# A four-layer graph network on one core: fourteen unread products per double step of the first layer

## The reference, cut to what matters

```python
h = jnp.maximum(_layernorm(x, axis=-1), 0.0)
# _L0_gnn_ref
msg = feat[src] * weight[:, None]
neigh_sum = jax.ops.segment_sum(msg, dst, num_segments=n)
deg = jax.ops.segment_sum(jnp.ones_like(weight), dst, num_segments=n)
h_neigh = neigh_sum / jnp.maximum(deg, 1.0)[:, None]
rst = feat @ W_self.T + b_self + (h_neigh @ W_neigh.T + b_neigh)
```

```python
d = jax.nn.gelu(layer_norm(x @ Wd1 + bd1, g1, b1), approximate=False)
d = jax.nn.gelu(layer_norm(d @ Wd2 + bd2, g2, b2), approximate=False)
```

## Time and profile before

| | us |
|---|---|
| median of 3 runs | 2665.58 |
| lowest and highest | 2657.37, 2678.04 |
| profiled execution, whole | 2675.34 |
| its span | 2673.3 |
| mean granted clock of TensorE in it | 0.738 |

### The profile page before, as it was taken

The page is one execution under the profiler, slowest core; times in us unless marked ns, Lnnn a source line. Parts: engine busy times, 40 slices in busy tenths (PEclk is TensorE's granted clock), DMA queues, the critical chain, the costliest instruction groups (busy, mean ns, idle before and its releaser), DMA issues.

```text
span 2673.3 us, 23453 instructions
## 1 busy us (share of the span) xinstructions
PE 1639.0 (61%) x7115; PEld 1239.3 (46%) x7115; DVE 1546.5 (58%) x2419; ACT 898.5 (34%) x1160; POOL 1327.1 (50%) x1404
## 2 busy tenths in 40 slices
PE   1456545545564365666567346878878634988892
PEld 1334334433453354544455234656656523767672
DVE  5445445544565376667677663555545834867783
ACT  1122122212221455555554312333333720433340
POOL 6545544554523545555555345554552034566653
PEclk7666666666665677777787767888988556989996
DMA  6112211211121344444444422323322621333332
GB/s 137 36 53 58 55 49 52 63 50 52 53 69 34 82 132 125 139 124 139 138 137 134 127 55 52 68 61 69 67 60 64 207 59 36 84 77 83 87 78 55
DMA packets 216506, 220.61 MB, mean 83 GB/s; under 512 B 107262, under 2 KB 170195, under 8 KB 216147
## 3 DMA queue, kind: packets, MB, share of 16 engines
q1 hardware_dynamic: 167635, 147.32, 18.6%
q0 software_dynamic: 45024, 58.36, 10.9%
q10 hardware_dynamic: 3744, 13.63, 1.3%
HBM read 117.72 MB, written 101.46 MB: 82 GB/s over the span
## 4 chain that ended last, share of the span: by engine, by line
PE 28%; issue 11%; DVE 11%; another core or an unknown queue 10%; ACT 7%; POOL 2%; DMA 1%; DVEq 0%; POOLq 0%; ACTq 0%; SPq 0%
PE psum L974 18%; POOL arena L655 2%; PE psum L999 2%; PE psum L1005 1%; DVE spare L1896 1%; DVE scan_ring L1896 1%; ACT arena L1204 1%; ACT arena L1231 1%; ACT arena L1283 1%; PE psum L1066 1%; DVE arena L1762 1%; PE psum L881 1%; PE psum L988 1%; ACT spare L1242 1%
## 5 line engine op out<-in xcount | busy, mean ns | idle before, releaser
L622 POOL DMA_INDIRECT gathered<-table,idx x1272 | 1210.1, 951 | 1084.0 <-issue 366.8
L1729 DVE COPY_PREDICATED spare<-spare,psum 64x512 f32<-64x512 uint8 x294 | 216.4, 736 | 282.6 <-ACT spare L1330 188.7
L974 PE MATMUL psum<-rounded 128*128 128x512 f32 x1144 | 299.6, 415 | 59.4 <-issue 38.1
L759 PE MATMUL psum<-ident,arena 128*128 128x128 f32 x416 | 109.7, 415 | 279.3 <-ACT arena L1121 265.5
L974 PEld LDWEIGHTS psum<-rounded 128*128 128x128 f32 x1144 | 225.5, 200 | 118.6 <-issue 53.1
L1567 DVE TENSOR_REDUCE rs<-arena 128x16 f32<-128x1024 f32 x52 | 63.3, 1217 | 341.3 <-ACT arena L1125 323.8
L759 PEld LDWEIGHTS psum<-ident,arena 128*128 128x128 f32 x416 | 70.8, 208 | 354.6 <-ACT arena L1121 284.1
L655 POOL DMA_INDIRECT arena<-scan,rowidx x100 | 103.3, 1033 | 213.3 <-DMA scan<-ea 111.8
L1125 ACT ACTIVATE arena<-psum 128x1024 f32<-128x1024 f32 x52 | 53.2, 1023 | 458.6 <-remote 350.3
L1330 ACT ACTIVATE spare<-psum 64x512 f32<-64x512 f32 x82 | 48.4, 590 | 397.5 <-remote 209.0
L1204 ACT ACTIVATE arena<-psum 128x512 f32<-128x512 f32 x156 | 82.0, 597 | 199.2 <-remote 160.8
(11 more groups left out here) (275 smaller groups left out, 3483.9 us busy)
## 6 DMA issues: line engine op xcount, KB each, us to landing
scan<-arena SPq DMA_DIRECT2D x52, 768.0 KB
scan<-ostage SPq DMA_DIRECT2D x130, 256.0 KB, 2.3
gathered<-table,idx POOLq DMA_INDIRECT x1272
d_mlp<-arena ACTq DMA_DIRECT2D x26, 512.0 KB
arena<-d_mlp SPq DMA_DIRECT2D x52, 256.0 KB
ea<-in_edge_attr SPq DMA_DIRECT2D x104, 128.0 KB
spare<-src_row SPq DMA_DIRECT2D x98, 128.0 KB
spare<-src_quarter SPq DMA_DIRECT2D x98, 96.0 KB
```

The lines of the kernel that those rows point to most:

```text
L622: pool.indirect_dma_start(out=out[:, j, hf, :], out_offset=None, in_=tab[layer], in_offset=bass.IndirectOffsetOnAxis(ap=idx[:, j, hf * NCH ...
L759: last = nc.tensor.transpose(P[:, 4, j::J], mlp[layer][:, k * CH + j * 128:k * CH + (j + 1) * 128], ident[:, :])
L974: last = nc.tensor.matmul(P[:, bank + t, :], parts[layer][n][:, b:b + 2, :].rearrange("p b d -> p (b d)"), tile(layer, m, u)[:, hf * CH:(h ...
L1729: picked = v.copy_predicated(rows[m % 2][halves[hf], :], quarter[m % 2][halves[hf], q - 1, :], P[halves[q % 2], bank + q // 2, :])
```

## The change

A helper is added to TensorE's program. One call of it issues n products of the identity with the identity, repeated to 256 columns, into columns 0 to 255 of a bank. Nothing reads them, and each bank is filled anew by the transposes that come next.

```diff
+            def keep_busy(n, bank):
+                for _ in range(n):
+                    nc.tensor.matmul(P[:, bank, 0:256], ident[:, :], ident[:, :].unsqueeze(1).to_broadcast([128, 2, 128]),
+                                     start=True, stop=True, skip_group_check=True)
...
             def l0_in(i, k):
+                pe.wait_ge(S("scanned", 1 - k), n_scanned(0, i + k))
+                if k == 0:
+                    keep_busy(2, 5)
                 pe.wait_ge(S("L0 msg made", k), past(i + 1))
-                pe.wait_ge(S("scanned", 1 - k), n_scanned(0, i + k))
                 for j in range(J):
...
                     pe.wait_ge(S("gelu made"), past(g))
+                keep_busy(4, 4)
                 pe.wait_ge(S("norms1 made"), i + 1)
                 norm_transpose(0, 0)
                 l0_in(i, 0)
...
                     norm_transpose(1, 0)
+                pe.wait_ge(S("evacuated", 1), n_evacuated(0, i))
+                keep_busy(6, 6)
                 l0_in(i, 1)
...
                 l0_hist(i)
+                keep_busy(2, 6)
                 l0_out(i, 0)
```

## The result

The kernel with the change takes 2758.22 us (median of 4 runs, 2751.41 to 2763.53) beside 2661.47 us for the kernel before on the same chip (4 runs): a ratio of 1.0352, interval 1.0317 to 1.0386. It is 97 us slower. The forecast was 2785, or 119 us slower.

The account below looks back on a forecast made before the run. A ring of waits bounds the first layer's loop, 29.3 us a double step. Six products on it cost 103 us, uncovered double steps 15: 118 us on the 2665.6 median gives 2784, said as 2785; range 2680 to 2930.

Parts of the forecast that it names:

- the first case: The forecast as described: the change slows the kernel to 2785 us, own range 2690 to 2810; chance 0.50.
- The ring: First layer's loop: gather batch, late TensorE semaphore, TensorE's start, message k = 1, next batch; 28.1 to 30.3 us.
- The price of one product: Each added 256-column product on TensorE: 0.94 us at the low clock, 0.5 us at the high one.
- Six products on the ring: Four into bank 4, two into bank 5, behind TensorE's start: 5.7 us, less 1.5 slack in 19 double steps; 103 us.
- what the clock gives back: An earlier clock rise could shorten the six products and two transpose blocks; lower bound 0.7 us a double step, not taken.
- A granted clock that is high right behind the start: Sign in the profile after, right behind TensorE's start, that the ring is not as described; 0.5 was expected there.
- The scan waits for the message transposes nearly always: Expected in the profile after: VectorE's scan waits for L767 23 times, some 90 us.
- Eight products at nothing: Six into bank 6, two behind the counts: hidden under gathers, costing nothing; double steps without a batch cost 15 us together.
- The double step: Expected in the profile after: one double step of the first layer's loop takes 33.5 to 35 us, against 29.
- Held earlier: Rival: late semaphores follow the amount of TensorE work, so the last gelu is held too; 138 us more, 2923; chance 0.25.
- The clock wins: Rival: products in idle time keep TensorE's clock at 1.00, saving 4.5 to 5 us a double step; about 2570; chance 0.15.
- Nothing moves: Rival: unseen slack in the ring, TensorE's start and batch shift against each other; 2665 to 2685 us; chance 0.10.

Follow-up runs that it names:

- the narrow products: The change plus the explicit wait, its fourteen products 16 columns wide instead of 256: 2705.04 us beside 2628.34 for the kernel before, ratio 1.0270.

## Why the prediction was right, point by point

The sign, the place and most of the size came out as the first case had it: 2758 us, inside its own range of 2690 to 2810, 27 us below the number.

**The ring.** Right for the change, where TensorE's semaphore is released 3.0 to 3.2 us behind the last gather in every double step; in the kernel before it came ahead of the batch's end in 3 of 22. The kernel before with an explicit wait for the batch's end takes the same time (1.0004), and the added time is GpSimd's wait for the message, 311.3 against 219.4 us, in the same 23 places.

**The price of one product.** Right at the low clock: 3.78 us for four in the timeline at 584.30, 0.94 each, as worked out from the halves of the earlier trace rows; 0.48 to 0.5 behind the rise (the last six, 2.85 us at 595.22 in the same double step).

**Six products on the ring: 5.7 us less 1.5 of slack.** Too high. On TensorE, from its start to the end of the message transposes, it was 1.97 us and is 6.27 (medians of 22), so 4.3 were added and not 5.7, and of these 1.4 went into the slack, much as said. The term that was mis-sized is "what the clock gives back". I took nothing for it; the clock rises within the six products: the pair into bank 5 took 0.86 to 1.71 us (1.24 in the median), not 1.9, and the message transposes 0.60 to 0.65 instead of 1.06. They end 6.3 us behind TensorE's start, where 7.5 to 8 were forecast. A granted clock that is high right behind the start was named as a sign that the ring is not as described; it is high within 3.3 to 6.1 us, and the ring held all the same, so the sign was badly chosen. The earlier trace rows had shown 10.5 us at 0.56 and then 1.00, but in that stretch TensorE did other work than it does now. With the explicit wait these six cost 77 us alone, and 62 on top of the eight, where the sum had 103.

**The scan waits for the message transposes nearly always.** Partly: 23 times, but 71.6 us and not 90, for the same reason.

**Eight products at nothing.** Failed, though small: 33 us alone (the estimate, for the steps without cover, was 15). The cover was taken to be the batch: work that ends before the release costs nothing. But the release itself moves when TensorE has more instructions to complete, by 0.6 to 1.0 us in each double step, and another 0.5 us lies between copy and scan (3.57 against 3.03). With the ring's part the excess is smaller, 95 - 77 = 18 us.

**The sum.** 103 + 15 was forecast; 77 and 33 were measured alone, 95 together. By these runs two errors, of 26 and 18 us, have opposite signs and partly made up for each other. That the sum of 118 is within 21 to 23 us of the 95 and 97 measured is in part luck.

**The double step.** 33.5 to 35 us were said. The row pair 593.31 and 625.62 (next start of a batch) gives 32.3, below that, for the same reason.

**Held earlier.** The rival was true in what it described and not in its price. The gelu is held, 172.0 us in 21 places. But it is released while the batch still runs (at 606.11, when gathers run until 612.96), so what is queued behind it does not run after the batch; the 138 us for it were not paid. Its reason, an amount of TensorE work rather than the gathers alone, is half of the truth as the narrow products show.

**The clock wins.** The clock did rise, 0.63 to 0.75 in the loop, and in the change without late semaphores it is at 0.97. It paid for 1.4 us of the 5.7 on the ring. It did not win: the products come behind the wait and not in it.

**Nothing moves.** False with late semaphores, and true without them, 1.0014: there the gathers bound the loop.

## What to carry to other kernels

Unread products behind the wait that ends an idle stretch do not fill that stretch: in program order they are part of the work that others wait for, and here 14 of them, at 0.5 to 0.94 us, cost 3.5%. Whether they would pay ahead of that wait, in the idle stretch itself, no run here tried. Before a stage is said to hide work under a transfer, look at whether its semaphores come on time: count the waits with no releaser in the trace, and see what runs until they end. And a term that is "hidden because it ends before the release" is only free if the release does not depend on how much was issued.

## What the runs showed of the hardware

**Semaphores of TensorE that come late while GpSimd gathers.** In one kind of runs (the kernel before at 2628 to 2662 us) they arrive late, in the first layer's loop of the kernel before up to 14.2 us behind the end of the matmul, and the square starts 2.4 us behind the end of the batch of gathers in the median (between 5.2 ahead of it and 3.1 behind). In the other (2033 to 2040 us) there is none. The same program differs by 600 us, of which, in the change's case, more lies behind the first layer than in it. Nothing in the records of the runs tells which kind a chip will be: chip 0 gave both kinds, at two times. What causes it stays open.

**TensorE slowed without a semaphore.** With 205 instead of 151 instructions a double step, its last ones come at one matmul in 0.7 to 1.4 us while gathers run, where sixteen of them took 0.56 us before. At most 62 weight loads and matmuls lay between the end of one and its semaphore. With no late semaphores the same program has no such rows.

**The granted clock rises sooner than the earlier trace rows made it look.** In the kernel before, with TensorE's start at 576.83, a block of transposes is at the low clock 7.6 us behind it and the next at the high one:

```profile
576.83 1.11 PE L759 MATMUL psum<-ident,arena 128*128 128x128 f32 x4 [12.25 <-ACT arena L1121]
...
584.42 1.12 PE L759 MATMUL psum<-ident,arena 128*128 128x128 f32 x4
585.33 0.67 PE L767 MATMUL psum<-ident,arena 128*128 128x128 f32 x4
```

With the products as TensorE's first work the norm transposes at 3.3 to 3.6 us are at the low clock in 15 of 22 double steps (1.06) and at the high one in 6 (0.60), and the message transposes, at 4.6 to 6.1 us, are at the high one in all 22 (0.60 to 0.65). With the narrow ones they are at the low one at 3.3 us, and L751 behind them is too.
